# Writing out the loop over the batches of a fused cross-attention and expert-FFN kernel

## The reference, cut to what matters

```python
l  = layernorm(layernorm(x));  xn = layernorm(ctx)
q  = l @ W_q;  k, v = split(concat(xn, l) @ W_kv)          # 333 keys
attn = softmax(mask(rmsnorm(q) * SCALE @ rmsnorm(k).T))     # per head
x  = x + (attn @ v) @ W_out + b_out
h  = layernorm(x)
cw = top-2-of-8 router weights of h                         # grouped, sigmoid
x  = x + sum_e cw[e] * relu(h @ up[e]) ** 2 @ down[e] + relu(h @ up_s) ** 2 @ down_s
```

## Time and profile before

| what | value |
|---|---|
| median of 3 runs | 1362.79 us (1362.51 to 1364.13) |
| the profiled execution's own time | 1370.73 us |
| its span, first to last instruction | 1368.9 us |
| PE busy | 1286.9 us, 94% |
| DVE busy | 1022.7 us, 75% |
| ACT busy | 747.5 us, 55% |
| POOL busy | 539.4 us, 39% |
| mean granted TensorE clock | 0.984 |

### The profile page before, as it was taken

One profiled execution on the slowest core, in us unless ns is written; L12 is line 12 of the kernel. 1 busy time (PEld: TensorE's weight loads), 2 busy tenths in 40 slices (PEclk: granted clock), 3 DMA queues, 4 the chain that ended last, 5 costly groups with the idle time before them and its releaser, 6 DMA issues.

```text
span 1368.9 us, 33442 instructions
## 1 busy us (share of the span) xinstructions
PE 1286.9 (94%) x10176; PEld 1194.2 (87%) x10176; DVE 1022.7 (75%) x3465; ACT 747.5 (55%) x1701; POOL 539.4 (39%) x477
## 2 busy tenths in 40 slices
PE   3799999999999999999999999999999999999997
PEld 2788899898899898899898899888889889889986
DVE  3478777788777778777778877777877778877765
ACT  3465555565555565555565555555555556555552
POOL 4143443343443343344343343333444334444332
PEclk9599999999999999999999999999999999999998
DMA  4000000000000000000000000000000000000000
GB/s 137 11 12 20 19 18 0 18 18 18 18 18 0 18 18 18 18 18 8 10 18 18 18 18 8 10 18 18 18 18 13 5 18 18 18 18 18 0 9 16
DMA packets 28099, 24.20 MB, mean 18 GB/s; under 512 B 6640, under 2 KB 27536, under 8 KB 28080
## 3 DMA queue, kind: packets, MB, share of 16 engines
q1 hardware_dynamic: 27744, 23.83, 5.5%
q0 software_dynamic: 336, 0.14, 0.2%
HBM read 15.57 MB, written 8.39 MB: 18 GB/s over the span
## 4 chain that ended last, share of the span: by engine, by line
PE 68%; DVE 13%; issue 12%; ACT 4%; DVEq 1%; POOL 1%; DMA 1%; POOLq 0%; ACTq 0%
PE attn_ps L367 13%; PE up_ps L261 6%; PE up_ps L263 6%; PE up_ps L262 6%; PE down_ps L261 5%; PE attn_ps L356 5%; PE attn_ps L261 5%; PE attn_ps L262 4%; PE attn_ps L263 4%; PE down_ps L263 4%; PE down_ps L262 4%; DVE masked L815 4%; PE attn_ps L309 2%; ACT relu L649 2%; ACT relu_sb L644 1%
## 5 line engine op out<-in xcount | busy, mean ns | idle before, releaser
L1148 POOL TENSOR_TENSOR hid_lo<-relu,hid_hi 128x512 fp32r<-128x512 f32 x192 | 246.6, 1284 | 485.1 <-DVE hid_hi L957 485.1
L261 PE MATMUL down_ps<-down_hi,hid_hi 128*128 128x256 f32 x768 | 238.4, 310 | 17.7 <-POOL hid_lo L1148 16.1
L972 DVE SCALAR_TENSOR_TENSOR acc<-down_ps,route_w,acc 128x256 f32<-128x256 f32 x512 | 222.0, 476 | 22.4 <-PE down_ps L263 17.7
L261 PE MATMUL up_ps<-x_hi,up_hi 128*128 128x256 f32 x768 | 230.3, 300 | 1.2 <-ACT x_hi L633 1.0
L263 PE MATMUL down_ps<-down_hi,hid_lo 128*128 128x256 f32 x768 | 215.9, 281 | 0.0
L262 PE MATMUL down_ps<-down_lo,hid_hi 128*128 128x256 f32 x768 | 215.7, 281 | 0.0
L262 PE MATMUL up_ps<-x_lo,up_hi 128*128 128x256 f32 x768 | 215.5, 281 | 0.0
L263 PE MATMUL up_ps<-x_hi,up_lo 128*128 128x256 f32 x768 | 215.5, 281 | 0.0
L367 PE MATMUL attn_ps<-v_sb,probs_t 111*128 111x64 f32 x1536 | 205.7, 275 | 10.0 <-DVE row_max L815 9.3
L611 ACT ACTIVATE probs<-masked,neg_max,q_scale 128x333 f32<-128x333 f32 x256 | 167.8, 656 | 79.0 <-DVE neg_max L822 79.0
L367 PEld LDWEIGHTS attn_ps<-v_sb,probs_t 111*128 111x128 f32 x1536 | 194.7, 196 | 16.8 <-DVE row_max L815 15.6
(11 more groups left out here) (145 smaller groups left out, 2819.3 us busy)
## 6 DMA issues: line engine op xcount, KB each, us to landing
x_in<-in_x SPq DMA_DIRECT2D x32, 256.0 KB, 2.7
out<-acc SPq DMA_DIRECT2D x32, 256.0 KB, 2.2
c_in<-in_ctx SPq DMA_DIRECT2D x32, 77.0 KB
up_stage<-in_up_t SPq DMA_DIRECT2D x1, 1536.0 KB, 12.1
down_stage<-in_down_t SPq DMA_DIRECT2D x1, 1536.0 KB, 15.0
mask_in<-in_mask SPq DMA_DIRECT2D x32, 9.6 KB, 2.8
w_stage<-in_w_kv SPq DMA_DIRECT2D x1, 512.0 KB, 5.8
w_stage<-in_w_q SPq DMA_DIRECT2D x1, 256.0 KB, 5.1
```

The lines of the kernel that those rows point to most:

```text
L261: nc.tensor.matmul(out_ap, s_hi, m_hi, start=first, stop=False)
L972: nc.vector.scalar_tensor_tensor(acc[:, t, :], down_ps[:, (e + 1) % 2, t * D:(t + 1) * D], route_w[:, t, e:e + 1], acc[:, t, :], ALU.mult, ...
L1148: nc.gpsimd.tensor_tensor(hid_lo[:, p % HID_RING, :], relu2[:, p % 2, :], hid_hi[:, p % HID_RING, :], ALU.subtract).then_inc(hid_lo_done, 1)
```

## The change

The helper loses its engine argument and its hardware loop. All 32 steps are issued from Python with a plain number `b`, on all five engines. The order of the work, the buffers, the waits and the instructions that compute are as before. Every wait is now against a constant, every DMA address is fixed, and no stream has a register computation or a branch in a step. `b` being a number also in steps 2 to 30, the tests `isinstance(b, int) and b == 0` (or `b == 1`) give the same answer as before there.

```diff
-        def steps(eng, step):
-
-            step(0, False, True)
-            step(1, True, True)
-            with eng.Fori(2, B - 1) as b:
-                step(b, True, True)
-            step(B - 1, True, False)
+        def steps(step):
+            for b in range(B):
+                step(b, b > 0, b < B - 1)
...
-            steps(sp, step)
+            steps(step)
...
-            steps(pe, step)
+            steps(step)
...
-            steps(act, step)
+            steps(step)
...
-            steps(dve, step)
+            steps(step)
...
-            steps(pool, step)
+            steps(step)
```

## The result

| | before | after |
|---|---|---|
| median of 20 runs | 1371.03 us (1362.51 to 1373.41) | 1361.1 us (1354.15 to 1364.94) |
| profiled execution, span | 1370.73, 1368.9 us | 1355.97, 1353.5 us |
| mean granted TensorE clock | 0.984 | 0.990 |

The ratio of the times is 0.9932 (0.9913 to 0.9950): 0.7% or 9.3 us less. The forecast was a gain of 8.7 us, 0.6%, at 1354.1 us and in a range of 1350 to 1361.

The account below looks back on a forecast made before the run. PE, busy 1286.9 of 1368.9 us, was taken as the bound. Gains of 0.28 + 0.02 = 0.30 us a step, times 29 steps, made 8.7 us; 1362.79 - 8.7 = 1354.1 us, range 1350 to 1361.

Parts of the forecast that it names:

- Point 1: POOL's gap between `q_norm` and `q_scale`: register work there costs 0.08 us a step, shortening PE's first stall by that.
- Point 2: ACT's relu square: its 0.17 us wait gap is covered by POOL's `q_scale` and `x_res`, so gain nothing.
- Point 3: DVE from first to last mask: computed waits between dependent instructions cost 0.20 us a step.
- Point 4: Second part of the step, from the first product with v: gain between 0 and 0.08 us, taken as 0.02.
- Point 5: PE's own sequencer and branch, and SP's address computations: cost and gain 0.
- Point 6: Added instruction fetch in 28 more steps, about 84 and 56 blocks, 1.8 MB: delay taken as 0.
- Rival B: PE's fetches come late behind loads or stores: 27 us slower, 1381 us; chance 0.06.
- a taken branch: Loop branch stalling for a fetch each pass: 25 us more gain, 1329 us; within a larger-gain rival of chance 0.02.
- The sum: Steps 2 to 30: 0.28 + 0.02 = 0.30 us a step, times 29 steps = 8.7 us gain.
- the last step: Whole time without profiler: the 8.7 us gain taken off the runs' median, 1362.79, giving 1354.1 us.
- rival A: Register work is dear only while recorded: 1362.8 us, no change, if all; 1358.4 if half; chance 0.13 in full or near.

Follow-up runs that it names:

- only_pool: Kernel before with only POOL's 32 steps written out, the other engines keeping the loop; step 15 lasts 40.77 us, single run 1368.0 us.
- only_pe: Kernel before with only PE's 32 steps written out, the other engines keeping the loop; step 15 lasts 40.85 us, single run 1371.0 us.
- only_dve: Kernel before with only DVE's 32 steps written out, the other engines keeping the loop; step 15 lasts 40.65 us, single run 1358.9 us.
- only_act: Kernel before with only ACT's 32 steps written out, the other engines keeping the loop; step 15 lasts 40.84 us, single run 1363.3 us.

## Why the runs fall into two groups

Of the 20 runs of before 7 lie between 1362.5 and 1365.7 and 13 between 1370.4 and 1373.4; of the 20 of after 9 between 1354.2 and 1357.7 and 11 between 1361.0 and 1364.9. Group against group the medians differ by 7.9 (lower) and 9.2 us (upper). The mean granted clock of a run is 0.987 to 0.992 in the lower group and 0.981 to 0.986 in the upper.

The traces of the kernels without extra matmuls in step 0 are of two kinds as well (all but res_first, whose steps differ). In six of them (before, only_pool, only_pe, and three of the kernels further below) the clock from 31 to 67 us is granted at 0.53 to 0.57 and step 2 starts at 112.0 to 114.3; in five (after, only_dve, only_act and two further below) it is 0.80 to 0.81, and step 2 starts at 105.5 to 107.0. My theory was that this stretch alone makes the groups.

To try it, PE gets extra matmuls in step 0: 38 in the first kind of kernel below, 56 in the second. Both kinds were made from the loop and from the written-out kernel. The results of the extra matmuls are never read; they are overwritten before the FFN needs the bank.

```diff
+                def keep_busy(n):
+                    for _ in range(n if first else 0):
+                        nc.tensor.matmul(down_ps[:, 0, :], w_hi[:, 0, 0:P], w_hi[:, 0, 0:2 * D], start=True, stop=True)
...
                 sum_q_squares(b, first)
+                keep_busy(9)
...
                 score_pair(b, 1, experts)
+                keep_busy(26)
...
                     project_q(b + 1)
+                keep_busy(3)
...
# the 56: also, in ffn() of step 0, for up 3 to 5 and down 0 to 5
+                        keep_busy(2)
```

> The kernel before with 38 extra matmuls (128x512, results never read) in step 0, where PE waits for weights to be split: 9, 26 and 3 of them. They keep PE at work while its granted clock would fall. My theory for why the runs of one and the same kernel fall into two groups some 7 us apart, and why the base of my prediction was low: the low clock in step 0 lasts about 34 us in some executions and about 17 in others, and costs 0.5 us per us. Then here the low clock in step 0 is gone, the long group with it, the time is at or below the lower group of before (1363), 1350 to 1363, and the steps last 40.85 as before. Rival: the two groups have another cause (DMA, the end of the kernel): the spread stays at 7 to 9 us.

> The same 38 matmuls in the kernel with all steps written out. My theory: steps of 40.57, and the whole 8 us below warm_loop, 1342 to 1355, with a spread under 3 us. Rival: spread as before.

With 38 the forecast failed: the loop kernel ran in 1361.0 to 1371.3, the written-out one in 1354.3 to 1362.6, two groups as before. The low clock of the profiled warm_loop had moved, to the stretch from 48 to 65 us (0.51 there) with its many small matmuls. So the extra matmuls have to reach there. (The next text says this of warm_out; its own trace has the low clock for 3.4 us only, near 33 us.)

> The kernel with all steps written out and 56 extra matmuls (128x512, results never read) in step 0: 9, 26 and 3 as in warm_out, and 2 in each of 9 places between the transposes of the probabilities, where PE has only small matmuls. In warm_out the low stretch moved there instead of going. Theory: with these the granted clock stays at 1.0 from the scores of step 0 on in all executions, step 2 starts at 102 to 107 us, and the runs lie within 3 us of each other, at or below 1357. Rival: the two groups of runs have another cause and the spread of 8 us stays.

> The kernel before, with the loop, and the 56 extra matmuls in step 0. If the two groups of runs come from the low clock in step 0 alone, these runs lie within 3 us of each other too, and the change can be measured without them: warm2_loop less warm2_out_b is 29 x 0.28 = 8.1 us less 0.4 for the steps that are a little longer, 7.7 us; warm2_loop at 1363 to 1366. If the base of my prediction was low for another reason, the spread of 8 us is back.

> The written-out kernel with the 56 matmuls again, on the same chip as warm2_loop: 1354 to 1358, spread under 3 us, 7.7 us (0.56%) below warm2_loop.

The stretch from 31 to 67 us (step 0) in the kernels before, after, warm2_loop and warm2_out_b. Columns: busy time and count of PE, PEld, DVE, ACT, POOL, then the granted clock, DMA share, GB/s:

```profile
31.00:67.00 36.00, 26.84 (x125) 24.31 (x126) 18.19 (x46) 16.94 (x34) 5.51 (x5) 0.54 0.04 10
```

```profile
31.00:67.00 36.00, 25.22 (x178) 22.27 (x177) 24.94 (x67) 20.10 (x44) 9.45 (x9) 0.80 0.04 11
```

```profile
31.00:67.00 36.00, 35.62 (x213) 29.66 (x214) 22.96 (x61) 18.64 (x42) 11.95 (x8) 0.92 0.04 11
```

```profile
31.00:67.00 36.00, 34.59 (x212) 28.79 (x211) 22.47 (x60) 18.61 (x41) 8.85 (x8) 0.95 0.04 11
```

In the profiled execution of before the clock was granted at 0.54 over these 36 us, so at the lower of its two levels (1.2 GHz) nearly all the time; in that of after at 0.80. PE has little to do in this part of step 0: ahead of its third pair of scores it stands still for 5.9 us for a `row_max` of DVE (trace of before), and DVE is splitting the experts' weights until then. Within it the clock comes back at different times in executions of one kernel. With the 56 matmuls it is up for nearly all of it (0.92, 0.95, and 1.00 in warm2_out), and the runs lie together: warm2_out 1354.6 to 1357.1 (6 runs), warm2_out_b 1356.9 to 1358.3 (7), warm2_loop 1363.7 to 1366.9 (12). The kernel before, run beside them, kept its two groups: 5 and 6 of 11 runs beside warm2_out, 11 and 6 of 17 beside the other two. So the groups come from the clock in step 0, with and without the loop. Two numbers are a little outside what I had given: warm2_loop spreads over 3.3 us and not 3, and step 2 of warm2_out starts at 108.2 and not by 107. The matmuls cost 1 to 3 us: warm2_out_b is 1.1 us above the lower group of after, warm2_loop 2.6 above the lower group of the kernel before that was run beside it.

This gives the cleanest measure of the change: 1365.33 - 1357.25 = 8.1 us, 0.59%, on one chip. I had expected 7.7, and 29 x 0.28 is 8.1. What decides in which executions the clock comes back in step 0 stays open; I have seen the clock, not its reason.

## What POOL's chain covers, and what POOL does to DVE

My prediction held ACT's gap covered by POOL's `q_scale` and `x_res`. To take the cover away, `x_res` was moved; the first two ways failed and showed why.

```diff
# res_first: x_res (residual) ahead of q_scale
-                q_scales(b, first)
-                residual(b, first)
+                residual(b, first)
+                q_scales(b, first)
# res_late: x_res after hid_lo of pair 1
                 q_scales(b, first)
+                low(0)
+                low(1)
                 residual(b, first)
-                for p in range(4):
-                    low(p)
+                low(2)
+                low(3)
```

> All steps written out, and POOL computes x_res before q_scale instead of after it. My theory says POOL's chain q_scale, x_res, hid_lo sets PE's first stall and DVE's first mask: hid_lo of pair 0 starts some 0.5 us earlier (4.87 us into the step, bound by relu and cast), the second cast ends at 6.43 instead of 6.96, so that the masks and the first product with v come 0.5 us earlier: steps of 40.05. Rival: x_res at the head of the step holds DVE up (both read SBUF) and x2_lo comes later, up to 0.5 us, so that the step gains nothing: 40.5 to 40.7.

> All steps written out, and POOL computes x_res after hid_lo of pair 1. Same gain for hid_lo and the casts, 0.5 us, but x_res then runs from 7.8 to 9.1 us into the step beside DVE's small router steps. If these are not held up: steps of 40.05. If they are held for what POOL takes, as the cast is now: 0.3 to 0.8 us is lost again, 40.3 to 40.8.

res_first took 1410 us, far worse than both expectations: 17 of the steps 2 to 30 last 41.85 (one of them 41.98), and the other 12 some 43.1, 1.27 more. In each of these 12 the trace has a stretch of 3.4 us at the lower level of the clock, in the others none. So of the 52 us by which these 29 steps are longer than in the kernel after, 37 come with the 41.85 and 15 with the dips of the clock. res_late took 1362, steps of 40.78, at the upper end of its second case. POOL and DVE of step 20 in res_late:

```profile
848.81 1.28 POOL L1120 TENSOR_TENSOR x_res<-x_in,bout_row 128x512 f32<-128x512 f32 x1
```

```profile
849.21 0.93 DVE L899 TENSOR_TENSOR biased<-score,gbias 128x16 f32<-128x16 f32 x1
```

and ahead of step 20 in res_first:

```profile
867.99 2.65 DVE L863 TENSOR_SCALAR x_hat<-x,mv,rstd 128x256 f32<-128x256 f32 x2 [0.29 <-POOL rstd L1101]
...
868.90 1.27 POOL L1120 TENSOR_TENSOR x_res<-x_in,bout_row 128x512 f32<-128x512 f32 x1
```

In res_late an addition of 16 elements, 0.18 us otherwise, takes 0.93: it ends 0.05 us after POOL's `x_res` does (850.14 and 850.09). In res_first the two `x_hat` take 2.65 instead of 0.73 and end 0.47 after `x_res`; PE waits 42.4 us in 32 steps for them, where it waited 1.9 in the kernel after. The masks and the subtractions, which read PSUM, keep their 0.5 and 0.4 us beside POOL. One thing stays open: the first `x_hat` of res_first starts 0.91 us before `x_res` does and needs 0.41 alone, so by these rows it should have been done. The only POOL instruction beside it at its start is a `k_scale` of 4 elements, and beside the same `k_scale` in the kernel after it takes 0.41. The next kernel, res_gap, has POOL wait for DVE's second `k_rms`, so that `x_res` falls on work that reads PSUM; res_gap2 also keeps `hid_lo` of pair 2 off the router's comparisons; res_gap_act_loop is res_gap with ACT in its loop.

```diff
+                pool.wait_ge(k_rms_done, b * 2 + 2)
+                residual(b, first)
                 q_scales(b, first)
-                residual(b, first)
... (low(0) to low(3) follow, as before)
# res_gap2, ahead of low(2):
+                if experts:
+                    pool.wait_ge(router_step, (b - 1) * ROUTER_STEPS + 15)
```

> All steps written out; POOL computes x_res before q_scale, but only once DVE's second k_rms is done (0.0 us into the step), so that it runs from 0.0 to 1.3 while DVE subtracts from PSUM. Theory: POOL's work holds up those DVE instructions that only touch SBUF (cast, x_hat, the router's), and not the ones that read PSUM; and POOL's chain sets the first stall. Then hid_lo of pair 0 starts at 4.87, the first mask at 6.46 as in res_late, nothing is held at 8.1, and the first product with v comes 0.5 us earlier than in the written-out kernel: first part 15.57, steps 40.05. Rival (any DVE instruction is held by POOL): x2_lo and the FFN's first matmul come up to 0.9 us later, steps 40.5 to 41.

> res_gap, and POOL's hid_lo of pair 2 also waits until the router's comparisons (L924, L925) are done. Theory: the 1.40 us of the first of them is 0.28 of work and 1.12 of being held by hid_lo; the last mask then comes another 1.0 us earlier, PE's stalls before the transposes of the probabilities and before the first product with v shrink to nothing or nearly: first part 14.6 to 15.0, steps 39.1 to 39.5, the whole 1305 to 1322 us in the profile. Rival: the comparison is slow by itself (four-dimensional operands): steps 40.05 as in res_gap or longer by the later hid_lo.

> res_gap with ACT alone back in its loop. My prediction said that ACT's register work is covered by POOL's chain and would be worth up to 0.2 us a step without that cover. Here POOL is free when the relu square is done, so the 0.17 us gap should show: steps of 40.22, 0.17 more than res_gap. Rival (ACT's work never matters): as res_gap.

Starts of steps 20 and 21 on PE in res_gap, res_gap2 and res_gap_act_loop:

```profile
826.25 0.26 PE L317 MATMUL attn_ps<-ident,k_rms 111*128 111x111 f32 x1
...
866.28 0.26 PE L317 MATMUL attn_ps<-ident,k_rms 111*128 111x111 f32 x1
```

```profile
821.34 0.26 PE L317 MATMUL attn_ps<-ident,k_rms 111*128 111x111 f32 x1
...
860.74 0.26 PE L317 MATMUL attn_ps<-ident,k_rms 111*128 111x111 f32 x1
```

```profile
835.81 0.26 PE L325 MATMUL attn_ps<-ident,k_rms 111*128 111x111 f32 x1
...
875.99 0.26 PE L325 MATMUL attn_ps<-ident,k_rms 111*128 111x111 f32 x1
```

Steps of 40.03 (expected 40.05), 39.40 (39.1 to 39.5) and 40.18 (40.22). So with `x_res` out of the way a step is 0.54 us shorter, and ACT's register gap of 0.17 then costs 0.15 (0.13 as the mean of steps 2 to 30): the cover was real.

But it was not what I had taken it for. The rows of `x_res` and of DVE's cast `hid_hi` (the first of a step) in the kernels before, only_act and res_gap; those of after are shown above:

```profile
649.02 1.28 POOL L1124 TENSOR_TENSOR x_res<-x_in,bout_row 128x512 f32<-128x512 f32 x1
649.85 0.73 DVE L957 CAST hid_hi<-relu 128x512 fp32r<-128x512 f32 x1 [0.87 <-ACT relu L649]
```

```profile
641.54 1.28 POOL L1128 TENSOR_TENSOR x_res<-x_in,bout_row 128x512 f32<-128x512 f32 x1
642.24 0.87 DVE L961 CAST hid_hi<-relu 128x512 fp32r<-128x512 f32 x1 [0.73 <-ACT relu L653]
```

```profile
830.61 0.43 DVE L953 CAST hid_hi<-relu 128x512 fp32r<-128x512 f32 x1 [0.57 <-ACT relu L645]
```

The cast starts 4.66, 4.53 and, in the kernel after, 4.37 us into the step, and takes 0.73, 0.87 and 0.95 us. The sooner ACT lets it start, the longer it takes: it ends 0.28 or 0.29 us after `x_res` in all three kernels, in every step from 2 to 30. Away from `x_res`, in res_gap, it takes 0.43. And POOL is not busy when `hid_lo` could start: it stands idle for 0.36 us, waiting for this cast. So what covered ACT's gap is that `x_res` holds DVE's cast, not that POOL had no time for `hid_lo`. It is also where most of DVE's 12 us of added busy time come from. The 0.52 us by which the cast is shorter in res_gap than in the kernel after is nearly all of the 0.54.

The comparison L924, in the kernel after and in res_gap2, each with POOL's `hid_lo`:

```profile
645.10 1.40 DVE L924 TENSOR_TENSOR above<-in_group 128x128 f32<-128x128 f32 x1
```

```profile
645.06 1.28 POOL L1144 TENSOR_TENSOR hid_lo<-relu,hid_hi 128x512 fp32r<-128x512 f32 x1 [3.03 <-DVE hid_hi L953]
```

```profile
832.21 0.29 DVE L924 TENSOR_TENSOR above<-in_group 128x128 f32<-128x128 f32 x1
...
832.79 1.29 POOL L1144 TENSOR_TENSOR hid_lo<-relu,hid_hi 128x512 fp32r<-128x512 f32 x1 [3.65 <-DVE tied L925]
```

0.29 us is its work, 1.1 us was being held. In res_gap2 the hold falls on a smaller step of the router instead (L927, 0.75 us instead of 0.28). res_gap2 runs in 1325.0 us (ratio to before 0.969, 0.9657 to 0.9723); I had given 1305 to 1322 for the whole. Five of its six runs lie between 1324.7 and 1326.1 and one at 1316.8: the two groups again.

The last two are res_gap2 with the loop of before put back on every engine (res_gap2_loop), and res_gap2 written out with the 56 extra matmuls of step 0 (best):

```diff
# res_gap2_loop (steps() gets its engine argument back)
+            step(0, False, True)
+            step(1, True, True)
+            with eng.Fori(2, B - 1) as b:
+                step(b, True, True)
+            step(B - 1, True, False)
-            for b in range(B):
-                step(b, b > 0, b < B - 1)
```

> The kernel before, with its loop, and POOL's two changes of res_gap2. With POOL's chain and the held comparison gone, DVE's and ACT's register work is still in front of the masks: steps 0.2 to 0.45 us longer than res_gap2's 39.40, 39.6 to 39.85; the register work is worth as much as before or more. Rival: PE has no stall left to hide it behind or to show it, and both last 39.40.

> res_gap2 with the 56 matmuls in step 0, all written out: steps of 39.40, no low clock in step 0; 1316 to 1321 in every run, 3.5% below the kernel before.

Starts of steps 20 and 21 in res_gap2_loop:

```profile
831.34 0.26 PE L321 MATMUL attn_ps<-ident,k_rms 111*128 111x111 f32 x1
...
871.31 0.26 PE L321 MATMUL attn_ps<-ident,k_rms 111*128 111x111 f32 x1
```

39.97 us, 0.57 more than res_gap2 and more than I expected (0.2 to 0.45). The register work that costs 0.28 in the kernel before costs twice that once the holds are gone. Its first mask comes 6.77 us into the step and 6.46 in res_gap2, 0.31 apart where it was 0.08, and from first to last mask it takes 8.60 and 8.32, 0.28 apart where it was 0.20. The kernel that joins all, best, runs in 1321.1 us (1320.1 to 1322.2, 5 runs; ratio 0.9665, 0.9633 to 0.9697), faster than both kernels of this case. Its steps are 39.39; its time is at the upper edge of the 1316 to 1321 that I gave.

## Why the prediction was right or wrong

- Point 1, POOL's `q_scale`, 0.08: right. The gap is 0.08 in step 15, and only_pool alone gives 0.08.
- Point 2, ACT at nothing: right in size, wrong in its reason. only_act gives nothing, and with the cover gone the gap costs 0.13 to 0.15, where I had said up to 0.2. But "The cover is POOL, which is busy with `q_scale` and `x_res` until then" does not hold: POOL is idle for 0.36 us ahead of `hid_lo`, and it is DVE's cast that `x_res` holds until 0.28 us after its own end. That the size came out was in part luck.
- Point 3, DVE 0.20: right; only_dve gives 0.20, with 8.96 us from first to last mask.
- Point 4, 0.02 of the second part: the part is 24.48 in step 15, as in the loop, so the term is 0; step 2 had supported that. The cost of the choice is 0.6 us.
- Point 5, PE and SP: right. only_pe leaves step 15 at 40.85, and the four engines' shares add up to the whole without SP.
- Point 6, fetch at nothing: right to 0.3 us in all. Steps 2 to 30 last 40.55 to 40.57, except steps 4 (40.66), 6 (40.64) and 25 (40.70). Steps 4 and 6 are like the longer steps that loop kernels without fetches have too. Step 25 is another matter: it is also long with only DVE written out (40.78 against 40.65), in warm_out and in warm2_out_b (40.69), each time with DVE's second `k_rms` 0.15 us late, and that `k_rms` is on time in every kernel looked at whose DVE loops. So it comes with DVE's written-out stream and costs 0.13 us once; that a fetch is its cause is not shown. 82 and 63 packets came, about as forecast. Rival B's 27 us did not come.
- The Trainium skill (Runtime: NRT & Kernel Launch, Instruction fetch mechanics) has a taken branch force a fetch when its target is outside the current window of two pages. By my working in the prediction that would have made the gain 25 us larger. The gain was 8.1, and the loop of before fetched one packet in 1140 us, though PE's body took three blocks of 16 KB the first time: the code of each engine's loop stayed on the core.
- The sum, 0.30 x 29 = 8.7: measured 7.8 in the steps of the two traces, 8.1 without the clock's groups, 9.3 (6.9 to 11.9) by the ratio.
- What failed is the last step, "taking the same amount off it gives 1362.79 - 8.7 = 1354.1". It took the median of three runs as the kernel's time. The profiled execution was 7.9 us slower, and I named that difference only in rival A, as the cost of recording. It was neither recording nor small noise: the three runs all fell in the lower group and the profiled one in the upper. The clock row of step 0, 0.54 for 36 us, was there to be read, and I did not read it: I looked at steps 1 to 31 alone. From the profiled execution's own time the same sum gives 1362.0, 0.9 above the median measured and 0.4 below the median of the upper group of after (1362.4). The range ended 0.1 us below the result; it had been drawn for the gain and not for the base.
- By how little it missed is luck, and a hit would have been too. The median of runs in two groups goes to the group that has the majority: 13 of 20 runs of before were in the upper one, and in a later set 11 of 17 were in the lower, with a median of 1363.3. One run more of after in the lower group would have put its median near 1359.4, inside the range, with the base just as wrong.
- Rival A fell: its ground, the 7.9 us, was the clock. The profiled executions (1370.73 and 1355.97) lie inside the groups of the other runs, so being recorded costs nothing that can be seen, and the gain is there in both groups (7.9 us in the lower, 9.2 in the upper).

## What to carry to other kernels

The loop's register work cost time here only where a chain of short dependent instructions on another engine ended in a wait of the bounding one. A step that is already written with constants, at the end of a loop, measures it before anything is built: here 16.37 against 16.09 gave the gain to 0.01 us a step. Compare the profiled execution with the runs before choosing a base, and where they differ by more than the change is worth, look for the clock at the start and end first and widen the range by that difference. When an engine is said to be covered by another, look which instruction ends last there and whether the other is idle before the next one. Large POOL instructions are best laid beside DVE instructions that read PSUM: that was worth 1.17 us a step here.

## What the runs showed of the hardware that I had not expected

- DVE is held by POOL: a DVE instruction on SBUF alone (cast, `x_hat`, the router's) that meets a POOL `TENSOR_TENSOR` of 128x512 elements ends 0.05 to 0.3 us after POOL's does, 0.18 us becoming 0.93, 0.29 becoming 1.40 and 0.43 becoming 0.95. Those that read PSUM are not held, and beside a `k_scale` of 4 elements `x_hat` kept its 0.41. Two POOL waits on this ground gave 1.17 us a step, four times the change of this case. Not every SBUF instruction was held: a reciprocal (L897) in res_late kept its 0.25 us beside `x_res`.
- In step 0 the clock is granted at one of its two levels for very different times in executions of one kernel, and that moves the whole by some 8 us.
- Computed waits can sit in front of an instruction for 0.08 us (POOL's `q_scale`) to 0.17 us (ACT's relu square), and both are gone with constants.
